# Attention with transposed scores, a row maximum taken ahead, and Q/K/V stored as two halves

## What is computed

```python
def _L0_xattn_ref(latents, context, Wq, Wk, Wv, Wo):      # H, KV, HD = 16, 4, 96
    hidden = jnp.concatenate([context, latents], axis=1)
    q = (latents @ Wq.T).reshape(b, q_len, H, HD)
    k = (hidden @ Wk.T).reshape(b, s_len, KV, HD)
    v = (hidden @ Wv.T).reshape(b, s_len, KV, HD)
    ...
    scores = jnp.einsum('bkgqd,bksd->bkgqs', q, k) * scale
    attn = jax.nn.softmax(scores.astype(jnp.float32), axis=-1).astype(q.dtype)
    out = jnp.einsum('bkgqs,bksd->bkgqd', attn, v)
    ...
    return out @ Wo.T
x = x + _L0_xattn_ref(_layernorm(x, axis=-1), ctx_4096, Wq, Wk, Wv, Wo)
x = x + _L0_ffn_ref(_layernorm(x, axis=-1), ...)
```

## Time and profile before

| what | us |
|---|---|
| three timed runs | 2343.84, 2348.21, 2352.84 (median 2348.21) |
| the profiled execution: its time | 2349.38 |
| its span, from the first to the last instruction | 2347.6 |
| stage 0, to the first products of stage A | 0 to about 96 |
| stage A | about 96 to 509.4 |
| Wo | 510 to 537 |
| stage B and the start of C | 537 to 1148.7 |
| stage C | to about 1420 |
| stages D and E | to the end |

### The profile page before, as it was taken

How to read it: one execution, slowest core, us unless ns; L and a number is a source line. 1 busy time by engine, 2 the same in 40 slices (tenths; PEclk the granted TensorE clock), 3 DMA queues, 4 the chain that set the end, 5 groups by cost and what they waited for, 6 DMA issues and landing times.

```text
span 2347.6 us, 33499 instructions
## 1 busy us (share of the span) xinstructions
PE 2270.2 (97%) x11500; PEld 1882.6 (80%) x11500; DVE 876.1 (37%) x1598; ACT 793.5 (34%) x1550; POOL 637.6 (27%) x468
## 2 busy tenths in 40 slices
PE   7899999988999999999999999999999979999997
PEld 7788888877888888888788877878787868888886
DVE  3401011016888888888400022312121032222332
ACT  4201111126777777777411122312122321111110
POOL 1000000004565655656322243301012422222221
PEclk9899999998999999999999999999999989999999
DMA  7312121242212212121233354422222443322222
GB/s 243 116 49 76 57 73 50 81 114 51 63 48 58 62 41 65 41 62 46 70 102 120 109 184 126 148 85 76 85 76 95 145 137 91 96 82 84 86 80 67
DMA packets 198446, 207.97 MB, mean 89 GB/s; under 512 B 31216, under 2 KB 145904, under 8 KB 198384
## 3 DMA queue, kind: packets, MB, share of 16 engines
q1 hardware_dynamic: 161104, 149.75, 21.5%
q10 hardware_dynamic: 37280, 57.42, 6.9%
HBM read 135.04 MB, written 72.09 MB: 88 GB/s over the span
## 4 chain that ended last, share of the span: by engine, by line
PE 92%; DMA 4%; DVE 1%; ACT 1%; issue 1%; POOL 0%; SPq 0%; ACTq 0%; DVEq 0%; POOLq 0%
PE psum L115 28%; PE psum L116 27%; PE psum L117 27%; PE psum L727 6%; PE psum L245 1%; DMA fold_scratch<-staging 1%; PE psum L170 1%; DMA operands<-h_scratch 1%; DMA staging<-in_wo 0%; DMA staging<-fold_scratch 0%; PE psum L1219 0%; PE psum L1218 0%; DMA staging<-in_up_w 0%; DMA staging<-in_expert_w 0%; DVE operands L946 0%
## 5 line engine op out<-in xcount | busy, mean ns | idle before, releaser
L115 PE MATMUL psum<-operands 128*128 128x512 f32 (+5 forms) x3208 | 1229.0, 383 | 26.5 <-POOL operands L1396 12.9
L116 PE MATMUL psum<-operands 128*128 128x512 f32 (+5 forms) x3208 | 1188.8, 371 | 0.0
L117 PE MATMUL psum<-operands 128*128 128x512 f32 (+5 forms) x3208 | 1187.4, 370 | 0.0
L115 PEld LDWEIGHTS psum<-operands 128*128 128x128 f32 (+3 forms) x3208 | 597.6, 186 | 173.2 <-issue 51.5
L117 PEld LDWEIGHTS psum<-operands 128*128 128x128 f32 (+3 forms) x3208 | 597.4, 186 | 107.9
L116 PEld LDWEIGHTS psum<-operands 128*128 128x128 f32 (+3 forms) x3208 | 598.7, 187 | 91.6
L670 POOL TENSOR_TENSOR operands<-operands 96x512 fp32r<-96x512 f32 (+3 forms) x112 | 129.7, 1164 | 561.4 <-ACT operands L663 561.4
L685 POOL TENSOR_SCALAR staging<-staging,small 128x576 f32<-128x576 f32 x126 | 216.2, 1727 | 191.6 <-DVE small L851 191.6
L862 DVE TENSOR_TENSOR operands<-psum,operands 128x512 fp32r<-128x512 f32 (+1 forms) x320 | 216.0, 678 | 31.4 <-ACT operands L803 31.3
L946 POOL TENSOR_TENSOR operands<-staging,operands 128x512 fp32r<-128x512 f32 x92 | 118.2, 1297 | 392.0 <-ACT operands L941 391.6
L845 DVE TENSOR_REDUCE small<-psum 128x1 f32<-128x576 f32 x256 | 192.6, 752 | 58.2 <-PE psum L117 58.2
(11 more groups left out here) (78 smaller groups left out, 929.0 us busy)
## 6 DMA issues: line engine op xcount, KB each, us to landing
h_scratch<-staging ACTq DMA_DIRECT2D x80, 256.0 KB, 2.2
operands<-h_scratch SPq DMA_DIRECT2D x64, 320.0 KB, 3.2
q_scratch<-staging ACTq DMA_DIRECT2D x48, 256.0 KB, 2.0
operands<-q_scratch SPq DMA_DIRECT2D x16, 768.0 KB, 6.0
o_scratch<-staging SPq DMA_DIRECT2D x64, 192.0 KB, 2.1
operands<-o_scratch SPq DMA_DIRECT2D x64, 192.0 KB, 2.5
staging<-in_wqkv SPq DMA_DIRECT2D x18, 512.0 KB, 6.3
staging<-in_x SPq DMA_DIRECT2D x4, 2048.0 KB, 8.0
```

The source lines that it names most:

```text
L115: e.matmul(o, lh, rh, start=first, stop=False)
L116: e.matmul(o, lh, rl, start=False, stop=False)
L117: return e.matmul(o, ll, rh, start=False, stop=last)
```

## The change

K, Q and V are split into high and low parts when they are evicted in stage 0 and stage A (ACT the high, DVE the low part), and both are stored, so stage B loads 8 tensors per group and splits none. Wo comes transposed from the host; its 12 blocks are loaded and split within the first 12 groups of stage B, and the transposes between A and B are gone.

Stage B per head is now: `mx`, 8 single products of 288 columns (high parts alone) for an approximate row maximum, which DVE reduces three heads ahead; `row`, one transpose of the 4 columns of negated maxima into a row, copied by DVE to `rowst` and put by a small DMA (`row_in`) into row 96 of Q, against a row of ones in K; `st`, 15 products of 512 columns that give the scores transposed, with the maximum subtracted; `exp` of 5 tiles on ACT; the split of the 5 tiles (high of tiles 0, 2, 4 by ACT and low by POOL; tiles 1 and 3 wholly by DVE, `split`); `pv`, 15 products of 512 columns with V widened by 32 columns of ones, so that rows 96 to 127 of its bank hold the sums. ACT evicts rows 0 to 95 (`out`), DVE takes the reciprocal of rows 96 to 127 (32x512, `recip`), three DMAs copy that to rows 0 to 95 (`spread`), POOL multiplies (`scale`), SP stores. The buffers of stage C's operand and of the first feed-forward weights move with it (`work_slot`), and one weight job moves from the end of stage C to the start of D.

```diff
-E = wo.shape[1]
+E = wo.shape[0]
...
-q_d = dram("q_scratch", (B * E, S))
+q_d = [dram(f"q_{h}_scratch", (B * E, S)) for h in ("hi", "lo")]
...
         for c in range(KC):
-            e.wait_ge(*past(c_ev, KC + 2))
-            e.dma_start(k_b[c * P:(c + 1) * P, :, S:T], stage[c][:, 0:BC].rearrange("p (b s) -> p b s", b=B)).then_inc(c_st, 16)
+            for i in range(2):
+                e.dma_start(k_b[i][c * P:(c + 1) * P, :, S:T],
...
         ctx_lo(e, 1)
+        for c in range(KC):
+            e.wait_ge(*past(c_sh, c + 1))
+            e.tensor_tensor(c_stage[c][1], PS[:, c, 0:BC], raw(c_stage[c][0]), ALU.subtract).then_inc(c_ev, 1)
         a_norm(e, 0)
+        for t in range(2):
+            e.wait_ge(*past(c_sh, KC + t + 1))
+            e.tensor_tensor(c_stage[KC + t][1], PS[:, 3 + t, 0:KVE], raw(c_stage[KC + t][0]), ALU.subtract).then_inc(c_ev, 1)
...
+def a_hi_out(e, b, n):
+    r = n % 3
+    w = NB if n < NQK else KVE
+    e.wait_ge(*past(a_acc, b * A_EV + n + 1))
+    e.wait_ge(*past(a_st[r], b * (32 * a_uses(A_EV)[r]) + 32 * (n // 3)))
+    e.activation(stage[r][0][:, 0:w], a_bank(n), ACT.Copy, scale=a_scale(n)).then_inc(a_sh, 1)
+def a_lo_out(e, b, n):
+    w = NB if n < NQK else KVE
+    e.wait_ge(*past(a_sh, b * A_EV + n + 1))
+    e.scalar_tensor_tensor(stage[n % 3][1][:, 0:w], a_bank(n), a_scale(n), raw(stage[n % 3][0][:, 0:w]),
+                           ALU.mult, ALU.subtract).then_inc(a_ev, 1)
...
+def a_act(e):
+    def body(b, last):
+        for n in range(A_EV):
+            if n == 9 and not last:
+                a_sqrt(e, b + 1)
+            if n == A_EV - 1 and not last:
+                for k in range(DK - 1):
+                    a_hi(e, b + 1, k)
+            a_hi_out(e, b, n)
+            if n:
+                a_store(e, b, n - 1)
+        if not last:
...
+def b_load_qk(e, g, p):
+    for i in range(2):
+        e.dma_start(raw(qp[p][i][0:HD, :]).rearrange("p (h s) -> p h s", h=G),
+                    q_d[i][bass.ds(g * (G * HD), G * HD), :].rearrange("(h p) s -> p h s", p=HD)).then_inc(b_qk[p], 16)
+        e.dma_start(raw(kp[p][i][0:HD, 0:T]), k_d[i][bass.ds(g * HD, HD), :]).then_inc(b_qk[p], 16)
...
+def b_sp_eng(e):
+    def row_in(i, o):
+        p, a = place(o)
+        r = o % 2
+        e.wait_ge(*past(b_rw, head(i, o) + 1))
+        e.sem_inc(idle, 1)
+        e.dma_start(raw(qp[p][0][HD:HD + 1, a * S:(a + 1) * S]).rearrange("o (u s) -> o u s", u=ST),
+                    raw(rowst[r])).then_inc(b_row[r], 16)
+    def spread(i, o):
+        r = o % 2
+        e.wait_ge(*past(b_rcp, head(i, o) + 1))
+        e.sem_inc(idle, 1)
+        e.wait_ge(*past(b_om, head(i, o) - 1))
+        e.sem_inc(idle, 1)
+        for c in range(3):
+            e.dma_start(rb[r][c * 32:(c + 1) * 32, :], ou[o % 4][HD:P, :]).then_inc(b_bc[r], 16)
+    def store(i, o):
+        e.wait_ge(*past(b_om, head(i, o) + 1))
+        e.sem_inc(idle, 1)
+        e.dma_start(o_d[bass.ds(head(i, o) * HD, HD), :], ou[o % 4][0:HD, :]).then_inc(b_os[o % 4], 16)
+    def load_wo(i, q):
+        c = i * 2 + q
+        e.wait_ge(*past(wo_lo, c))
...
+    def body(i, last, with_wo):
+        for hh in range(2 * G):
+            p, a = place(hh)
+            g = i * 2 + hh // G
+            if a == 0 and not (last and p == 1):
+                e.wait_ge(*past(b_pt, g * (G * NT)))
+                e.sem_inc(idle, 1)
+                b_load_v(e, g + 1, 1 - p)
+            if not (last and hh + 2 >= 2 * G):
+                row_in(i, hh + 2)
+            if a == G - 1 and not last:
+                e.wait_ge(*past(b_st, g * (G * NT) + G * NT))
+                e.sem_inc(idle, 1)
+                b_load_qk(e, g + 2, p)
+            if with_wo and a == 1:
+                load_wo(i, p)
+            if last and hh == G + 1:
+                c_first_loads(e)
+            spread(i, hh)
+            store(i, hh)
...
+def b_pool(e):
+    def lo(i, o, j):
+        k = {0: 1, 2: 2, 4: 3}[j]
+        e.wait_ge(*past(b_hia, head(i, o) * 3 + k))
+        e.tensor_tensor(pt[j][1], pst[(o * NT + j) % 4], raw(pt[j][0]), ALU.subtract).then_inc(b_lop, 1)
+    def scale(i, o):
+        r = o % 2
+        e.wait_ge(*past(b_bc[r], 48 * nth(i, o, 2) + 48))
...
+def b_pe(e):
+    def mx(i, o, u):
+        p, a = place(o)
+        if a == 0 and u == 0:
+            e.wait_ge(*past(b_qk[p], 64 * nth(i, o, 2 * G) + 64))
+        e.wait_ge(*past(b_mx, head(i, o) * ST + u - 1))
+        for h in range(2):
+            m = e.matmul(su[u % 2][:, h * TH:(h + 1) * TH], qp[p][0][0:HD, a * S + u * P:a * S + (u + 1) * P],
+                         kp[p][0][0:HD, h * TH:(h + 1) * TH], start=True, stop=True)
+        m.then_inc(b_S, 1)
+    def row(i, o):
+        e.wait_ge(*past(b_mx, head(i, o) * ST + ST))
+        e.wait_ge(*past(b_rw, head(i, o)))
+        e.transpose(PS[0:ST, 7, 0:P], nm[o % 2], ident[:]).then_inc(b_rt, 1)
+    def st(i, o, j):
+        p, a = place(o)
+        if j == 0:
+            e.wait_ge(*past(b_row[o % 2], 16 * nth(i, o, 2) + 16))
+        e.wait_ge(*past(b_ex, head(i, o) * NT + j - 1))
+        kh, kl = (t[:, j * P:(j + 1) * P] for t in kp[p])
+        qh, ql = (t[:, a * S:(a + 1) * S] for t in qp[p])
+        parts3(e, PS[:, 4 + (o * NT + j) % 2, :], kh, kl, qh, ql, True, True).then_inc(b_st, 1)
+    def pv(i, o, j):
+        p, a = place(o)
+        if j == 0:
+            e.wait_ge(*past(b_oe, head(i, o)))
+            e.wait_ge(*past(b_rcp, head(i, o)))
+            if a == 0:
+                e.wait_ge(*past(b_vl[p], 64 * nth(i, o, 2 * G) + 64))
+        if j % 2:
+            e.wait_ge(*past(b_lod, head(i, o) * 2 + (j + 1) // 2))
+        else:
+            e.wait_ge(*past(b_lop, head(i, o) * 3 + j // 2 + 1))
+        vh, vl = (t[:, j, :] for t in vp[p])
+        parts3(e, PS[:, 6, :], vh, vl, pt[j][0], pt[j][1], j == 0, j == NT - 1).then_inc(b_pt, 1)
+    def body(i, last, with_wo):
+        for hh in range(2 * G):
+            for j in range(NT):
+                if not (last and hh + 1 >= 2 * G):
+                    st(i, hh + 1, j)
+                if j < ST and not (last and hh + 3 >= 2 * G):
+                    mx(i, hh + 3, j)
+                pv(i, hh, j)
+                if j == 1 and not (last and hh + 2 >= 2 * G):
+                    row(i, hh + 2)
+    for u in range(ST):
+        mx(0, 0, u)
+    for u in range(ST):
+        mx(0, 1, u)
+    row(0, 0)
+    for u in range(ST):
+        mx(0, 2, u)
+    row(0, 1)
+    e.wait_ge(*past(b_cst, N_CST))
+    for j in range(NT):
+        st(0, 0, j)
...
+def b_act(e):
+    def exp(i, o, j):
+        m = head(i, o)
+        e.wait_ge(*past(b_st, m * NT + j + 1))
+        if j % 2:
+            e.wait_ge(*past(b_lop, m * 3 + {1: -1, 3: 0}[j]))
+        elif j < ST:
+            e.wait_ge(*past(b_lod, m * 2 + {0: -1, 2: 0}[j]))
+        else:
+            e.wait_ge(*past(b_lop, m * 3 + 1))
+        e.activation(pst[(o * NT + j) % 4], PS[:, 4 + (o * NT + j) % 2, :], ACT.Exp).then_inc(b_ex, 1)
+    def hi(i, o, j):
+        t = head(i, o) * NT + j
+        e.wait_ge(*past(b_ex, t + 1))
+        e.wait_ge(*past(b_pt, t + 1 - NT))
+        e.activation(pt[j][0], pst[(o * NT + j) % 4], ACT.Copy).then_inc(b_hia, 1)
+    def tiles(i, o):
+        exp(i, o, 0)
+        exp(i, o, 1)
+        hi(i, o, 0)
+        exp(i, o, 2)
+        exp(i, o, 3)
+        hi(i, o, 2)
+        exp(i, o, 4)
+        hi(i, o, 4)
+    def out(i, o):
+        e.wait_ge(*past(b_pt, head(i, o) * NT + NT))
+        e.wait_ge(*past(b_os[o % 4], 16 * nth(i, o, 4)))
+        e.activation(ou[o % 4][0:HD, :], PS[0:HD, 6, :], ACT.Copy).then_inc(b_oe, 1)
+    def wo_high(i, q):
+        e.wait_ge(*past(wo_ld, (i * 2 + q) * 16 + 16))
+        e.activation(wo_part(i, q, 0), wo_raw, ACT.Copy).then_inc(wo_hi, 1)
+    def body(i, last, with_wo):
+        for hh in range(2 * G):
+            if not (last and hh + 1 >= 2 * G):
+                tiles(i, hh + 1)
+            if with_wo and hh % G == 2:
+                wo_high(i, hh // G)
+            if last and hh == 2 * G - 1:
+                c_units_hi(e, 0)
+            out(i, hh)
...
+def b_dve(e):
+    def mx(i, o, u):
+        if u == 0:
+            e.wait_ge(*past(b_rt, head(i, o) - 1))
+        e.wait_ge(*past(b_S, head(i, o) * ST + u + 1))
+        e.tensor_reduce(nm[o % 2][:, u:u + 1], su[u % 2][:, 0:T], AX.X, ALU.max, negate=True).then_inc(b_mx, 1)
+    def row(i, o):
+        e.wait_ge(*past(b_rt, head(i, o) + 1))
+        e.wait_ge(*past(b_row[o % 2], 16 * nth(i, o, 2)))
+        e.tensor_copy(rowst[o % 2], PS[0:ST, 7, 0:P]).then_inc(b_rw, 1)
+    def split(i, o, j):
+        t = head(i, o) * NT + j
+        k = head(i, o) * 2 + (j + 1) // 2
+        e.wait_ge(*past(b_ex, t + 1))
+        e.wait_ge(*past(b_pt, t + 1 - NT))
+        e.tensor_copy(pt[j][0], pst[(o * NT + j) % 4]).then_inc(b_hid, 1)
+        e.wait_ge(*past(b_hid, k))
+        e.tensor_tensor(pt[j][1], pst[(o * NT + j) % 4], raw(pt[j][0]), ALU.subtract).then_inc(b_lod, 1)
```

(26 more changed lines are left out.)

564 lines of the change are left out of this document (227 added, 337 removed).

## The result

The changed kernel takes **2635.03 us** (median of 4 runs, 2627.2 to 2641.9) beside 2347.31 us for the kernel before on the same chip: a ratio of 1.122, with a 95% interval of 1.118 to 1.126. The profiled execution has a span of 2625.4 us. The direction of the forecast was right; its size was not (2393 us, range 2340 to 2550).

The account below looks back on a forecast made before the run. The prediction took the kernel to be bound by what PE issues per head. Stage B rises from 639.3 to 672 us: 2349.4 + 33 + 9.5 + 1.5 - 1.2 is about 2393 us, range 2340 to 2550.

Parts of the forecast that it names:

- PE's list: Stage B, TensorE's own work per head: 8 products of 288 columns, 30 of 512, one transpose, 8.25 us.
- Chain 1: Every head, ACT: next pv waits for out on bank 6; PE waits 0.46 us, plus 12 us for Wo rounding.
- the sum: Stage B's added terms: 13.5 + 64 x 8.7 + 12 - 4.5 + 77 + 17 = 672 us, against 639.3.
- Chain 2: Every head, DVE: 7 to 8.2 us of work with the reciprocal taken at 0.69 us, ending before out.
- the other bound: High bound for RECIPROCAL on 32x512: 9 ns an element, 4.7 us for 512.
- rival 2: Slow reciprocal in stage B: at 4.7 us pv waits, 12.4 us a head, 2523 us in all; chance 0.32.
- Chain 3: SP's queue, once a group: row_in lands late behind Q/K loads; PE waits 5.5 us in 14 groups, 77 us.
- Stage 0: 14 ACT store issues instead of 7 before line 254, which starts near 99.4; everything behind moves by 9.5 us.
- Stage A: Extra stores and DVE work fit under PE; a new batch's second bank is freed late three times, 1.5 us.
- Moved work in C and D: Moved weight job, work_slot and removed waits in C cost 0, under PE's work in D.
- rival 1: Stage B's large loads are hidden, so 77 and 17 us go: 2299 us; chance 0.18.
- rival 3: Faster by PE: all three chains slack and out early, 64 x 8.25 + 25, 2270 us; chance 0.02.

Follow-up runs that it names:

- best version: Version before the best one, with the maxima row transposed and copied sooner and Wo's subtraction on GpSimd in two halves: 2331.7 us, 0.992 of the kernel before.
- copy kernel: Changed kernel with line 969 copying the 32x512 sums instead of taking their reciprocal (division left out): 2468.9 us, 1.051 of the kernel before.
- queue open: Changed kernel with loads spread over heads and maxima row issued ahead of the store: 2343.4 us with a copy for the reciprocal, 2615.2 with the reciprocal.
- both SP edits and the copy: Changed kernel with loads spread over heads, maxima row ahead of the store, and a copy instead of the reciprocal (division left out): 2343.4 us, 0.998.
- both SP edits: Changed kernel with a group's loads spread over its heads and the maxima row issued ahead of the store on SP; reciprocal kept: 2615.2 us, 1.114.
- both SP edits and the spare matmuls: Changed kernel with loads spread, maxima row ahead of the store, and 16 extra 384-column matmuls ahead of each head's first pv product: 2504.1 us, 1.065.
- version before the best one: Kernel with reciprocal and its followers one head later (2633.0 us), with K, V, Q, Wo loads written one head earlier and ACT's Wo copy later: 2365.9 us, 1.007.

## Why the prediction was wrong, point by point

- **PE's list, 8.25 us a head: right.** In the best version PE is busy 477.28 of 520 us at clock 0.98, with 9.00 us a head: 8.26 us.
- **Chain 1: right in total, not in its spread.** In the copy kernel the waits at `pv` are mostly 0.7 to 1.1 us, not 0.46, ended by the eviction or the copy in turn, but only 47 heads have one. They make 42.5 us (those over 0.15 us), where the sum had 64 x 0.46 and 12 for Wo, 41 us.
- **Chain 2: the step that failed.** The reciprocal was taken at 0.69 us, since RECIPROCAL and TENSOR_SCALAR differed by 10 ns at one element and 8 ns at four. A pair of rows at one and four elements says nothing of 512. The term was 3.364 us, 6.25 ns a column, and the other bound, 9 ns, was nearer. The copy in its place gave 166 us back, and 2469 us would have been in the range; with the queue open it gave 272. This was rival 2, with 0.32. The Trainium skill's "repeat count of 8" ("VectorE: DVE Perf Modes", First, the fixed hardware budget) pointed the right way; at the 0.96 GHz that this page gives (Specifications), eight passes would be an estimate of 8.3 ns; the trace has 6.25. The rest of DVE's list was right: 392.33 us busy in 520 with both SP edits and the copy are 7.2 us a head, where 7 to 8.2 stood.
- **Rival 2's sum was short as well.** Between its 10.2 us a head at 2.5 us and its 12.4 at 4.7 lie 11.1 at 3.36; measured were 14.08, 3.0 more. It had no term for the clock: 1.87 us a head (13.85 to 11.98), 111 us in all. The prediction priced 14 gaps at 2.4 us and half of them at that, but not 64 gaps of 3.6 us. And "the row and the loads then have time" was only half true: both SP edits took 0.23 us a head (14.08 to 13.85). Most of the rest is the start of the reciprocal, which the sum had 0.23 us behind the last product. In the kernel with both SP edits and the spare matmuls (a product of `pv`, DVE's split of tile 3, the reciprocal):

```profile
688.88 0.39 PE L117 MATMUL psum<-operands 128*128 128x512 f32 x1
688.46 1.67 DVE L994 TENSOR_TENSOR operands<-staging,operands 128x512 fp32r<-128x512 f32 x1
690.16 3.36 DVE L999 RECIPROCAL staging<-psum 32x512 f32<-32x512 f32 x1
```

  The last product ends at 689.27, and the reciprocal starts 0.89 us later, because DVE is still at the split: 0.66 us a head. In the changed kernel, in 580 to 1100 us, the reciprocal also stands directly behind the split in every head (as at 696.73 in the timeline above, 1.3 us behind the end of the product).
- **Chain 3: right in kind, its sizes too small.** With the copy TensorE waits 7.7 us on average in 14 groups for the row behind spread, scaling, store and V's loads, where 5.5 was forecast. Of the 2.2 us between, 1.5 are the path from the end of the scaling to the row: 5.8 us (725.95 to 731.77), where the sum had 4.3 (18.6 to 22.9; the last DMA was priced at 1.4 us there, and at 2.1 in an ordinary head). The fixed part of 1.3 us in the price of the loads stands in no row; the 192 KB in 2.1 us and the 984 KB in 6.4 us of the earlier trace rows give about 1.1. Both SP edits gave 126 us where 77 and 17 stood; with the long reciprocal they gave 20. The step missed that the same path has only 0.7 us to spare in an ordinary head, so that spreading the loads is not enough.
- **The 76 us by which the copy kernel passed 2393** are these sizes: its 63 head periods took 719.9 us, the sum 649.6 (63 x 8.7 + 12 - 4.5 + 77 + 17). The waits for the row were 111 us instead of 77, and TensorE's time outside of its waits was 562 us instead of 532 (515 for its list and 17 for the clock), at clock 0.90: the clock was priced too low here too.
- **Stage 0: forecast 9.5 us, measured 1.1, part of it chance.** Stage A's first product starts at 99.06 instead of 97.99, and line 254 at 91.43 instead of 89.94, not at 99.4. The 14 issues took 9.0 us from 82.4 on, where 10.5 stood, and the normalization ended at 81.4 instead of 86.3. This end varies: in the profiles of all 18 kernels with the new stage 0, line 254 starts between 91.4 and 98.0, at 94.5 in the middle. Stage A was right within 2 us. Moved work in C and D: right, no change.
- **The chances.** Slower at 0.72 was right, and not only by the reciprocal: with the short copy the kernel is slower too (1.051), by chain 3. The range ended at 2550 although the slow reciprocal stood at 2523 without a clock term, and so left out the likeliest way to be worse. Added up again, rival 1 is 2298 us and rival 3 is 2273, which changes nothing.

## What to carry to other kernels

An instruction whose price is known only at one or four elements has no price at 512: bound it by its slope, and if the high bound changes the answer, keep that instruction off the path that frees a PSUM bank. A wait put into every iteration of a loop on TensorE is to be priced twice, as the wait and as the clock behind it. When two chains run beside each other, each experiment on one alone shows little; the four corners of both edits tell what they hold together, and a queue's list is to be read to its end for every small transfer that waits behind another engine.

## What the runs showed of the hardware

- RECIPROCAL on 32 partitions, f32: 1.764 us for 256 columns, 3.364 for 512, from PSUM, and 3.348 from SBUF (median, best version). A copy of the same 512 took 0.696 us.
- After the idle 3.63 us TensorE's products of 512 columns ran from 700.28 to 701.40 at 2.4 GHz (0.23 us apart) and only then at 1.2 GHz (0.43 us apart), until 704.0; after the next gap, 3.35 us, they began at 1.2 GHz (712.63). With spare work in the gaps the granted clock was 1.00 again.
- DVE's cast of 128x512 takes 0.43 us alone, 1.25 on average in the changed kernel's stage B, and up to 8.7 us (991.32 to 1000.02) in the version before the best one, where GpSimd worked without a pause from 988.6 to 999.7. That the shared port is the cause is argued from their overlap, and no run separates it.
- The broadcast of the reciprocal (three DMAs of 64 KB, each 2.0 us in the median of the changed kernel) landed 9 us after its issue behind 1.97 MB in the same queue.
